# Two lone chunks instead of three beside the paired chunks of the last two feed-forward items

## The reference

```
x = x + 0.5 * ffn(layernorm(x))
x = x + mamba2(layernorm(x))     # 64 heads of 16, state 128, in_proj, conv of 4, gated norm, out_proj
x = x + 0.5 * ffn(layernorm(x))
ffn(x): x = fwht(x * SU_ug)/64; h = silu(x @ W_gate.T * s1) * (x @ W_up.T * s2)
        h = fwht(h * SU_dp)/64; return h @ W_down.T * s3       # 512 -> 2048 -> 512
```

## Time and profile before

| | |
|---|---|
| median of 3 runs | 1649.05 us (1648.89 to 1649.43) |
| profiled execution, its own time | 1650.64 us |
| its span, first to last instruction | 1648.9 us |
| PE busy | 1615.0 us (98%), x9612 |
| DVE, ACT, POOL busy | 1087.8 (66%), 660.8 (40%), 459.6 us (28%) |
| mean granted clock of TensorE | 0.995 |
| chain that ended last, PE's share | 69% |

### The profile page before, as it was taken

How to read it: one execution, slowest core, us unless ns; L and a number is a source line. 1 busy time by engine, 2 the same in 40 slices (tenths; PEclk the granted TensorE clock), 3 DMA queues, 4 the chain that set the end, 5 groups by cost and what they waited for, 6 DMA issues and landing times.

```text
span 1648.9 us, 25148 instructions
## 1 busy us (share of the span) xinstructions
PE 1615.0 (98%) x9612; PEld 1304.5 (79%) x9612; DVE 1087.8 (66%) x2096; ACT 660.8 (40%) x988; POOL 459.6 (28%) x365
## 2 busy tenths in 40 slices
PE   7999999999999999999999999999999999899999
PEld 4788888878888778888778888877888877678887
DVE  7544445675677777777776768777775775665543
ACT  5334343464433463333454333355333341343321
POOL 1666662012212212212212222222131221543400
PEclk9999999999999999999999999999999999999999
DMA  7855555654454444454444444445444435432334
GB/s 285 303 201 206 215 192 204 230 182 153 159 167 163 137 160 152 152 171 144 154 163 149 157 165 152 158 146 183 146 166 162 161 106 178 141 128 90 128 101 155
DMA packets 230886, 274.76 MB, mean 167 GB/s; under 512 B 14064, under 2 KB 190320, under 8 KB 222192
## 3 DMA queue, kind: packets, MB, share of 16 engines
q1 hardware_dynamic: 230768, 273.15, 49.3%
HBM read 222.79 MB, written 50.33 MB: 166 GB/s over the span
## 4 chain that ended last, share of the span: by engine, by line
PE 69%; DVE 5%; ACT 2%; issue 2%; DMA 1%; POOL 1%; SPq 0%; ACTq 0%; DVEq 0%; POOLq 0%
PE bank L1263 23%; PE bank L1219 12%; PE bank L1306 10%; PE bank L1431 5%; PE bank L1343 5%; PE bank L1320 3%; PE bank L1500 3%; PE bank L1471 2%; PE bank L1487 2%; PE bank L1449 2%; PE bank L1494 1%; PE bank L1459 1%; DMA cum_stay<-m_aS 1%; DVE res L2044 1%; DVE xT L2018 0%
## 5 line engine op out<-in xcount | busy, mean ns | idle before, releaser
L1263 PE MATMUL bank<-fxT,wj 128*128 128x512 f32 x1608 | 381.5, 390 | 0.0
L1263 PEld LDWEIGHTS bank<-fxT,wj 128*128 128x128 f32 x1608 | 301.6, 188 | 62.8
L1219 PE MATMUL bank<-xT,wi 128*128 128x512 f32 x900 | 225.8, 399 | 1.5 <-DVE m_cv L2127 0.5
L1306 PE MATMUL bank<-m_wd,m_hb 128*128 128x512 f32 x864 | 218.0, 395 | 3.6 <-DVE res L2044 2.7
L1219 PEld LDWEIGHTS bank<-xT,wi 128*128 128x128 f32 x900 | 168.2, 190 | 40.3 <-issue 5.0
L1306 PEld LDWEIGHTS bank<-m_wd,m_hb 128*128 128x128 f32 x864 | 161.1, 189 | 37.9 <-DVE res L2044 3.8
L1734 ACT CAST m_hb<-xn 128x512 fp32r<-128x512 f32 x76 | 47.1, 620 | 342.8 <-DVE xn L2031 334.9
L2492 POOL TENSOR_TENSOR m_L<-m_L,m_GT 128x512 f32<-128x512 f32 x36 | 52.7, 1463 | 436.7 <-ACT m_L L1788 436.7
L2044 DVE TENSOR_TENSOR res<-bank,res 128x512 f32<-128x512 f32 x148 | 101.9, 689 | 34.6 <-PE bank L1306 32.5
L1788 ACT ACTIVATE m_L<-bank 128x512 f32<-128x512 f32 x128 | 76.5, 598 | 86.8 <-PE bank L1449 86.5
L2031 DVE SCALAR_TENSOR_TENSOR xn<-bank,sc,xn 128x512 f32<-128x512 f32 x76 | 56.7, 746 | 68.1 <-PE bank L1263 68.0
(11 more groups left out here) (279 smaller groups left out, 2742.0 us busy)
## 6 DMA issues: line engine op xcount, KB each, us to landing
wj<-ug_split SPq DMA_DIRECT2D x155, 512.0 KB, 4.2
m_wd<-dn_split SPq DMA_DIRECT2D x43, 1024.0 KB, 4.9
wi<-in_split SPq DMA_DIRECT2D x76, 512.0 KB, 3.3
ug_split<-b_wu SPq DMA_DIRECT2D x8, 2048.0 KB, 14.2
m_wo<-out_split SPq DMA_DIRECT2D x32, 512.0 KB, 4.1
in_split<-b_msp SPq DMA_DIRECT2D x20, 512.0 KB, 3.8
wi<-ug_split SPq DMA_DIRECT2D x17, 512.0 KB, 4.2
raw<-in_wug SPq DMA_DIRECT2D x8, 1024.0 KB, 6.9
```

The source lines that it names most:

```text
L1219: ins = pe.matmul(to[:], w[:, a, k, :], xT[:, b, k, :], start=(k == 0 and i == 0), stop=(k == KH - 1 and i == 2))
L1263: ins = pe.matmul(to[:], w[:, a, k, :], frm[:, b, k, :], start=(k == 0 and i == 0), stop=(k == KH - 1 and i == 2))
L1306: ins = pe.matmul(F[t % 2][:], hb[:, a, j, ck(t)], w[:, b, j, :], start=(j == 0 and n == 0), stop=(j == 1 and n == 2))
```

## The change

`SOLO` becomes 2, so `PAIRED` 6 and `UNITS` 12: the second lone chunk of item `BATCH` is the last before the units, and two lone chunks of item `ITEMS - 1` follow them. With it the code around unit 0 is arranged anew:

- the last `out_proj` writes the banks A, X, Y and S[1] (`last_out_bank`) in place of F[1], F[0] in turn; its `s_oa` waits go, waits for `s_L`, `s_ex`, `s_y`, `s_st` come in front;
- the two root steps that stood before the first chunk's `add_down` stand behind it, the transposes of the last item behind `up1`;
- the downs of the last lone chunk use F[0], F[1], S[0], S[1] (`solo_bank`), and all four stand between unit 0's products 2 and 3; two of the rows' turned banks are S[0] and S[1], so its tiles 2 and 3 wait for `row_differences`; the third turned row is in bank A for all items;
- `tf[2]`, `tf[3]` and all low parts of the rows are VectorE's (`third_difference`, `fourth_difference`, `sums_of_rows_low`), in unit 0, in the order `SPLIT`; the products wait for them one by one (`SPLIT_UP`);
- GpSimd's sums for unit 0 wait for `s_fs`, so they start behind the roots; `load_pair_down(0)` waits for the fourth difference.

```diff
     ITEMS = BATCH + 2
-    SOLO = 3
+    SOLO = 2
     PAIRED = NC - SOLO
...
     PRODUCTS = 7
+    SPLIT = (1, 0, 2, 3)
+    SUMMED = (TPG, TPG, TPG + 3, TPG + 5)
+    SPLIT_UP = (TPG + 2, TPG + 1, TPG + 4, TPG + 6)
     order = [BI_DT, BI_B, BI_C] + [i for b in range(NB) for i in (NB + b, b)]
...
-            return (S[0], S[1], A if i < BATCH else Y, X)[t]
+            return (S[0], S[1], A, X)[t]
...
             return hb1[:, p % 2] if g else hb[:]
+        def solo_bank(t):
+            return (F[0], F[1], S[0], S[1])[t]
+        def last_out_bank(t):
+            return (A, X, Y, S[1])[t]
...
                 if x == 0:
-                    sp.wait_ge(s_tp, TPG + 2)
+                    sp.wait_ge(s_tv, SUMMED[3])
                 elif x <= PAIRED + 1:
...
-            def up0(at, pairs=0):
+            def up0(at):
                 wait(pe, s_acc, downs(at) - 1)
-                wait(pe, s_oa, TPG * pairs)
                 half_up(4 * place_of(at) + 1, F[0]).then_inc(s_u, 1)
...
                     pe.wait_ge(s_hl, 4 * p + 3 + g)
-                pe.wait_ge(s_acc, pair_downs(p, g) + t - 3)
+                pe.wait_ge(s_acc, pair_downs(p, g) + t - 3 if p or g else pair_downs(p))
                 for j in range(2):
...
                     pe.wait_ge(s_lo, 2 * at + 2)
-                    pe.wait_ge(s_tv, TPG)
-                elif t == 2:
                     pe.wait_ge(s_h, 2 * at + 2)
+                elif t == 1:
                     pe.wait_ge(s_sil, 2 * at + 2)
+                else:
+                    pe.wait_ge(s_tv, t - 1)
                 for j in range(2):
                     for n, (a, b) in enumerate(PASSES):
-                        ins = pe.matmul(banks[4 + t][:], hb[:, a, j, ck(t)], wd[:, b, j, :], start=(j == 0 and n == 0), stop=(j == 1 and n == 2))
+                        ins = pe.matmul(solo_bank(t)[:], hb[:, a, j, ck(t)], wd[:, b, j, :], start=(j == 0 and n == 0), stop=(j == 1 and n == 2))
                 ins.then_inc(s_d, 1)
...
                     pe.wait_ge(s_hd, 2 * (u - 2) + 1)
-                else:
-                    pe.wait_ge(s_L, QUADS * MIXED)
+                elif u:
+                    pe.wait_ge(s_tv, TPG)
+                else:
+                    pe.wait_ge(s_pev, LGATE * BATCH)
                 product(x_bank, a11, b11, True)
...
                     pe.wait_ge(s_cc, 3 * (u - 2) + 3)
-                else:
+                elif u:
                     pe.wait_ge(s_tv, TPG)
+                else:
+                    pe.wait_ge(s_oa, TPG * NPAIR * BATCH)
                 product(y_bank, a12, b21, True)
                 if u == 0:
-                    part(0)
-                    part(1)
+                    for t in range(TPG):
+                        part(t)
                 pe.wait_ge(s_sl, u + 1)
-                pe.wait_ge(s_tv, TPG + 2)
+                pe.wait_ge(s_tv, SPLIT_UP[1])
                 pe.wait_ge(s_sn, 4 * u + 1)
                 product(x_bank, s2, t2, False)
-                part(0 if u else 2)
+                if u:
+                    part(0)
                 pe.wait_ge(s_cc, 3 * u + 1)
+                pe.wait_ge(s_tv, SPLIT_UP[0])
                 product(y_bank, s1, t1, True)
-                part(1 if u else 3)
-                pe.wait_ge(s_tp, TPG + 3)
+                if u:
+                    part(1)
+                pe.wait_ge(s_tv, SPLIT_UP[2])
                 pe.wait_ge(s_sn, 4 * u + 2)
...
                 pe.wait_ge(u_loaded, u_count)
-                pe.wait_ge(s_tv, TPG + 3)
+                pe.wait_ge(s_tv, SPLIT_UP[3])
                 pe.wait_ge(s_sn, 4 * u + 4)
...
                 pe.wait_ge(s_yl, 2 * (pair + 1))
+                if pair == NPAIR * BATCH - 1:
+                    pe.wait_ge(s_L, QUADS * MIXED)
+                    pe.wait_ge(s_ex, MIXED)
+                    pe.wait_ge(s_y, MIXED)
+                    pe.wait_ge(s_st, MIXED)
                 for t in range(TPG):
-                    if t >= 2:
+                    if pair == NPAIR * BATCH - 1:
+                        to = last_out_bank(t)
+                    else:
+                        to = F[1 - t % 2]
+                    if pair == NPAIR * BATCH - 1:
+                        pass
+                    elif t >= 2:
                         pe.wait_ge(s_oa, TPG * pair + t - 1)
-                    elif pair == NPAIR * BATCH - 1:
-                        pe.wait_ge(s_acc, downs(at) - t)
                     elif t == 0:
...
                         for n, (a, b) in enumerate(PASSES):
-                            ins = pe.matmul(F[1 - t % 2][:], yh[:, (2 * pair + i) % 4, a, ck(t)], wout[i][:, b, :],
+                            ins = pe.matmul(to[:], yh[:, (2 * pair + i) % 4, a, ck(t)], wout[i][:, b, :],
                                             start=(i == 0 and n == 0), stop=(i == 1 and n == 2))
...
                     out_proj(NPAIR * BATCH - 1, at)
-                up0(at, NPAIR * BATCH if at == MIXED else 0)
+                up0(at)
                 gate1(at)
-                if at == MIXED + SOLO - 2:
+                up1(at)
+                if at == MIXED + 1:
                     for t in range(TPG):
                         beside_turn(ITEMS - 1, t)
-                up1(at)
                 if at < MIXED + SOLO - 1:
...
                 else:
-                    act.wait_ge(s_tv, TPG + 3)
-                    act.wait_ge(s_tp, TPG + 3)
+                    act.wait_ge(s_tv, SPLIT_UP[3])
                 act.copy(pair_hidden(p, g)[:, 0, j, :], four(u)[:, g, :]).then_inc(s_hh, 1)
...
-                if i < 2:
-                    act.wait_ge(s_tv, TPG)
-                else:
-                    act.wait_ge(s_tp, TPG + i - 1)
+                act.wait_ge(s_tv, SUMMED[i])
                 act.copy(tb[:, 0, i], tf[:, i]).then_inc(s_th, 1)
...
             hidden_high(at, 0)
+            silu(at, 1)
             for t in range(TPG):
                 beside_row(ITEMS - 1, t)
-            silu(at, 1)
             for t in range(TPG):
                 beside_turn(ITEMS - 1, t)
-            hidden_high(at, 1)
-            at = MIXED + 2
-            silu(at, 0)
-            sums_of_rows_high(0)
-            sums_of_rows_high(1)
-            sums_of_rows_high(2)
-            hidden_high(at, 0)
-            silu(at, 1)
-            sums_of_weights_high(0)
             hidden_high(at, 1)
...
                     paired_high(u - 1, 1)
+                else:
+                    sums_of_weights_high(0)
+                    for i in SPLIT[:3]:
+                        sums_of_rows_high(i)
                 snapshot(u, 1, 3, x_bank)
+                if u == 0:
+                    sums_of_rows_high(SPLIT[3])
                 paired_silu(u, 0)
-                if u == 0:
-                    sums_of_rows_high(3)
                 snapshot(u, 3, 4, y_bank)
...
                 dve.wait_ge(s_d, TPG * (MIXED + SOLO - 1) + t + 1)
-                dve.tensor_tensor(r, banks[4 + t][:], r, ALU.add).then_inc(s_acc, 1)
+                dve.tensor_tensor(r, solo_bank(t)[:], r, ALU.add).then_inc(s_acc, 1)
...
+            def third_difference():
+                dve.wait_ge(s_tv, TPG)
+                dve.tensor_tensor(tf[:, 2], tf[:, 1], bf[:, 0:2], ALU.subtract).then_inc(s_tv, 1)
+            def fourth_difference():
+                dve.wait_ge(s_tv, TPG)
+                dve.tensor_tensor(tf[:, 3], bf[:, 2:4], tf[:, 1], ALU.subtract).then_inc(s_tv, 1)
             def sums_of_rows_low(i):
...
-                dve.wait_ge(s_th, i + 1)
+                dve.wait_ge(s_th, 1 + SPLIT.index(i))
                 dve.tensor_tensor(tb[:, 1, i], tf[:, i], tb[:, 0, i].bitcast(F32), ALU.subtract).then_inc(s_tv, 1)
...
                 dve.wait_ge(s_op, TPG * pair + t + 1)
+                frm = last_out_bank(t) if pair == NPAIR * BATCH - 1 else F[1 - t % 2]
                 if pair % NPAIR:
-                    dve.tensor_tensor(acc[:, t, :], F[1 - t % 2][:], acc[:, t, :], ALU.add).then_inc(s_oa, 1)
-                else:
-                    dve.tensor_copy(acc[:, t, :], F[1 - t % 2][:]).then_inc(s_oa, 1)
+                    dve.tensor_tensor(acc[:, t, :], frm[:], acc[:, t, :], ALU.add).then_inc(s_oa, 1)
+                else:
+                    dve.tensor_copy(acc[:, t, :], frm[:]).then_inc(s_oa, 1)
...
             next(other)
-            next(other)
             at = MIXED + 1
...
             next(other)
+            hidden(at, 0)
+            next(other)
             bias(1, s_fs)
-            hidden(at, 0)
             hidden_low(at, 0)
+            hidden(at, 1)
             for t in range(TPG):
                 beside_turn(ITEMS - 1, t)
-            row_differences(0)
-            hidden(at, 1)
             hidden_low(at, 1)
-            at = MIXED + 2
             for t in range(TPG):
-                add_down(at - 1, t)
-                if t < TPG - 1:
-                    row_differences(t + 1)
-            sums_of_rows_low(0)
+                row_differences(t)
```

(31 more changed lines are left out.)

## The result

The changed kernel takes 1637.2 us (median of 4, 1635.39 to 1637.54) against 1649.24 us (4 runs): ratio 0.9924, 95% interval 0.9907 to 0.9941. That is faster by 12.0 us; the forecast was 1641.9 us, 7.15 us faster. Run again later (e8_after_again) it took the same 1637.2 us, beside 1646.94 us of the kernel before on that chip: ratio 0.9946 (0.9932 to 0.9959), 9.7 us faster. The profiled execution has a span of 1635.6 us.

The account below looks back on a forecast made before the run. TensorE was taken to bound the kernel except for a 79.67 us stretch around the first paired unit. Unit 0 ending earlier (-19.95), added work (+13.80) and unit 1 (-1.0) made -7.15 us: 1641.9 us, range 1637.0 to 1646.5.

Parts of the forecast that it names:

- +13.80 us behind unit 0: After the first paired unit: two more units of 15.10 us, one lone chunk of 16.40 less, +13.80 us.
- the chunk count, -2.6 us: Whole kernel, before any waits: moving one chunk of each of the last two items to paired form saves 2.6 us.
- the first term: Ahead of up0 after the last output projection: the 0.83 us wait goes, but only 0.5 us is kept.
- The second lone chunk, the transposes, the solo downs: Before unit 0's third product: roots hidden, transposes wait until 1406.3, solo downs to 1414.9 almost without a wait.
- Low(1): 2.33: Unit 0, VectorE's low-part subtraction for part 1: slowed beside GpSimd to 2.33 us from 1.22; product 3 waits 1.5.
- Third difference 2.33: Unit 0, VectorE's third row subtraction: slowed beside GpSimd to 2.33 us, ending at 1421.75.
- For 6 and 7 I charge 2.2 us: Unit 0's last two products: a clock drop after the waits costs 2.2 us, so the unit ends at 1432.9.
- 1.0 us less: Unit 1: 1.0 us less than the earlier 10.93, as VectorE catches up during slow products 6 and 7.
- (a): Rival for unit 0: no slowing of VectorE and no clock drop, 1637.1 us; chance 0.22.
- (b): Rival for units 0 and 1: upper bounds of waits and clock, 1647.0 us; 0.12 still faster, 0.08 same.
- (c): Rival: the clock stays at 1.2 GHz after unit 0's waits, through units 1 and 2, 1666 us; chance 0.03.
- (d): Rival for the whole kernel: waits stay as before, only the work's -2.6 us, 1646.4 us; within a 0.08 chance.

Follow-up runs that it names:

- e8_after_again: Changed kernel, unchanged, run and profiled once more; 1637.2 us, ratio 0.9946 to the kernel before on that chip.
- e5: Changed kernel with three lone chunks again (SOLO = 3), the rest of the arrangement kept; 1641.35 us.
- e9: Changed kernel with the last output projection back in banks F[1] and F[0] and up0 waiting for the adds; 265.34 us from last projection to end.
- e1: Changed kernel with the first half of the root chain put back ahead of the first lone chunk's add_down; 1642.0 us, median of ten.
- e3: Changed kernel with GpSimd's sums of weights for unit 1 held until the third difference is done; 1637.81 us.
- e2: Changed kernel without GpSimd's wait behind the roots before unit 0's sums of weights; 1638.29 us.
- e0: Kernel before the change, unchanged, profiled once more; 275.61 us from last projection to end, against 275.72.
- e6: Changed kernel with third difference ahead of low(0), ScalarE's fourth cast later, GpSimd's unit 1 sums held until low(2); 1638.18 us.

## Why the prediction was right and where it was not

- **The work.** Right: +13.80 us behind unit 0 was measured as +13.76; the chunk count, -2.6 us, as -2.55 between e5 and e8, whose clocks went alike (-2.9 between e5 and the profile after).
- **The projection and the first lone chunk.** Right in kind: no wait ahead of `up0`, none over 0.2 us ahead of the downs or between them, no clock drop. The size of the first term was off: 0.5 us was kept by the forecast, 1.2 us by the runs (e9), since the 1.29 us of `hidden_low` was carried over from the earlier trace rows and it took 0.69. `up0` of the second lone chunk starts 22.5 us behind the projection, 27.8 before: 5.3 us, that is the forecast's 4.5 and the 0.7 just named. e1 shows the order of the roots as the cause.
- **The second lone chunk, the transposes, the solo downs.** Right within 0.1 us once the 0.7 is taken off.
- **The step that failed: "Low(1): 2.33", "low(0) 2.33"**, the median of the earlier trace rows given to every subtraction near GpSimd. Measured: 1.23 and 1.75 us; the "Third difference 2.33" was right with 2.32. Of the 3.1 us by which product 4 came earlier than forecast, these two terms are 1.7, the projection's term is 0.7, and some 0.5 are the row differences, which ended that much earlier still. VectorE and GpSimd in the kernel after, and ScalarE's two instructions ahead of product 6's release:

```profile
1410.96 1.23 DVE L2094 TENSOR_TENSOR m_tb<-m_tf,m_tb 128x1024 fp32r<-128x1024 f32 x1
1411.11 2.26 POOL L2579 TENSOR_TENSOR m_gu<-wj 128x512 f32<-128x512 f32 x1 [5.40 <-DVE m_sb L2099]
...
1412.70 1.75 DVE L2094 TENSOR_TENSOR m_tb<-m_tf,m_tb 128x1024 fp32r<-128x1024 f32 x1
1413.33 2.29 POOL L2581 TENSOR_TENSOR m_gu<-wj 128x512 f32<-128x512 f32 x1
...
1414.38 2.32 DVE L2085 TENSOR_TENSOR m_tf<-m_tf,m_bf 128x1024 f32<-128x1024 f32 x1
...
1418.98 1.75 DVE L2089 TENSOR_TENSOR m_tf<-m_bf,m_tf 128x1024 f32<-128x1024 f32 x1
...
1420.76 1.05 ACT L1802 CAST m_tb<-m_tf 128x1024 fp32r<-128x1024 f32 x1 [2.49 <-DVE m_tf L2089]
1421.71 0.72 ACT L1778 ACTIVATE m_qs<-m_qs,sc 128x512 f32<-128x512 f32 x1
```

Low(1) starts 0.15 us ahead of GpSimd and runs its 1.23 us; GpSimd's operation takes 2.26, and ends about 1.2 us behind low(1)'s end. Low(0) starts at 1412.70 and ends 1.08 us behind the end of that operation (1413.37); the third difference starts at 1414.38, inside the next one (to 1415.62), and ends 1.08 behind it. The fourth difference (1418.98, 1.75 us) ends 1.09 behind GpSimd's operation of 1418.05 to 1419.64. Each waits for the operation under way, and no longer. That is what the Trainium skill, SBUF — State Buffer, section "SBUF: two separate sides", states: the port pair is an exclusive lock, the one that starts first has it for the whole instruction. The trace agrees, with these numbers and with 2.32 in e3, which ends 1.08 behind as well; a doubling of both would have given 2.4 for low(1) too. The prediction quoted the rule and valued it at 0.4 us at most; it had weighed it only for a subtraction that comes second, although in its own walk low(1) starts at 1414.0, the moment at which GpSimd is released. VectorE's adds that read a bank were not slowed: 0.68 us at 1416.62, inside GpSimd's operation of 1415.70 to 1417.29.
- **Products 5 to 7, the second term that was mis-sized.** The waits of the chain are there, 2.88 and 1.01 us for 3.5 and 2.1. "For 6 and 7 I charge 2.2 us" was wrong for the profile after, where the clock was back before product 6, and nearer in e8, e5, e2 and e1 (1.6, 1.5, 1.9 and 2.5 us over the 3.18 of products 6 and 7 after). By the start of unit 1 the forecast was 5.3 us late: 3.2 for all up to product 6 and 2.1 for the clock.
- **Unit 1.** "1.0 us less" came out as 1.3 in e8 (9.62), where the clock had been low, and as 0.1 in the profile after, where it had not. The two terms go together, as the forecast had it; their sum was charged as +1.2 us and is 0 in the profile after and 0.3 in e8. So from the start of the projection 4.4 us were missed in all: 3.2 up to product 6, 1.2 by the clock's two terms.
- **The rest of the gap.** The span (1635.6) is 6.15 us under the forecast's 1641.75; 1.73 of them lie ahead of the change and are luck of that execution (e0).
- **The rivals.** (a), no slowing and no clock drop, 1637.1 us, came nearest in number (11.95 us for 11.57), but not as it was meant: two of the three subtractions were slowed and the clock did drop in product 5. These costs were mostly met by the projection's 0.7 us and the row differences' 0.5, which (a) did not have. (b), (c) and (d) did not come.

What stays open: why the same 2.88 us wait drops the clock in one execution and not in another (e9, 1.00 throughout; after, product 5 alone; e8, into product 7), and what sets the wait for the cumulative rows. Also, no run takes apart what removed the 4.60 us idle stretch of the earlier trace rows, the largest of the waits before. In the kernel before it ended with the low part of the hidden rows, on VectorE:

```profile
1438.31 5.08 PE L1336 MATMUL bank<-m_wd,m_hb 128*128 128x512 f32 x12 [4.69 <-DVE m_hb L2037]
```

There `hidden_low(at, 1)` stood behind the low part of the weights' sums (1432.99, 2.31 us) and itself took 2.82 us, with GpSimd at work all the time. In the changed code it stands ahead of the row differences and of that low part, and took 0.68 us (at 1406.00), with GpSimd idle. That this is the cause is read from the order of the code and the two traces, not tested by a run.

## What to carry to other kernels

Where two engines make each other wait, as VectorE's subtractions and GpSimd's sums do here, walk through them as a queue: who starts first pays nothing, who starts second pays the rest of the operation under way, and the median of a few such rows is no price for any one of them. When a shared engine is held back to protect a chain, look for who reads its result one step on; here it cost more than it saved (e6) or just as much (e3). Measure a local change from a point just ahead of it: from there two profiles of a kernel agreed within 0.4 us, while their spans were up to 2.7 us apart.

## What the runs showed that was not expected

The start of the last projection varied by 5.1 us over the thirteen profiles, beside a gain forecast as 7.15. Two things go with it: the waits for the cumulative rows, the first of them from 0.35 to 3.04 us long, and the granted clock from 352 to 380 us, from 0.88 to 1.00. And a low clock in a stretch that is bound by other engines costs little: product 5 at half speed for 1.3 us more took 1.3 us off the wait behind it (e9 against after, 2.28 and 1.01), and the following unit gave back 1.2 of the 1.6 us that products 6 and 7 had lost (e8).
